# Decoder with two cross attentions: turned scores with the maximum subtracted in the product, low parts of the probabilities on VectorE

## The reference

```python
q = (query @ Wq + bq); k = (bank @ Wk + bk); v = (bank @ Wv + bv)
scores = einsum('bhqd,bhkd->bhqk', q, k) / sqrt(hd)
attn = softmax(scores, axis=-1)
out = einsum('bhqk,bhkd->bhqd', attn, v)
return out @ Wo + bo
```

## Time and profile before

| | |
|---|---|
| median of 3 runs | 2616.53 us (2615.01 to 2621.03) |
| span of the profiled execution | 2613.8 us |
| its mean granted clock | 0.934 |
| busy: PE, VectorE, ScalarE, GpSimd | 2432.4, 1110.8, 947.7, 585.1 us |
| first attention, second attention | 105 to 766 us, 1127 to 1789 us |

### The profile page before, as it was taken

One profiled execution on the slowest core, in us unless ns is written; L12 is line 12 of the kernel. 1 busy time (PEld: TensorE's weight loads), 2 busy tenths in 40 slices (PEclk: granted clock), 3 DMA queues, 4 the chain that ended last, 5 costly groups with the idle time before them and its releaser, 6 DMA issues.

```text
span 2613.8 us, 38193 instructions
## 1 busy us (share of the span) xinstructions
PE 2432.4 (93%) x14208; PEld 2160.2 (83%) x14208; DVE 1110.8 (42%) x2206; ACT 947.7 (36%) x1892; POOL 585.1 (22%) x397
## 2 busy tenths in 40 slices
PE   4899999999977789699999999998999999999997
PEld 3788888888866667588888888887999999999997
DVE  7455545555457368444556455654640000200022
ACT  2444434454443144343454344533222222311130
POOL 4111101110132634311111011101222222222222
PEclk9899999999978878789999999998999999999998
DMA  3000000000021010100100000000111111111111
GB/s 136 1 24 24 15 8 23 23 23 6 22 81 29 1 44 0 60 1 28 28 27 21 6 27 27 32 1 33 64 48 65 56 64 56 56 56 64 56 57 41
DMA packets 29513, 93.60 MB, mean 36 GB/s; under 512 B 3752, under 2 KB 4008, under 8 KB 29320
## 3 DMA queue, kind: packets, MB, share of 16 engines
q1 hardware_dynamic: 29448, 92.72, 11.0%
HBM read 91.07 MB, written 1.64 MB: 35 GB/s over the span
## 4 chain that ended last, share of the span: by engine, by line
PE 86%; DVE 6%; ACT 3%; POOL 3%; issue 2%; DMA 0%; DVEq 0%; SPq 0%; POOLq 0%; ACTq 0%
PE psS L272 18%; PE psS L274 16%; PE psS L273 16%; PE psT L1337 7%; PE psJ L272 4%; PE psJ L273 4%; PE psJ L274 4%; PE psO L272 4%; PE psO L274 3%; PE psO L273 3%; PE psT L272 2%; PE psT L274 2%; PE psT L273 2%; DVE x_res L884 1%; DVE stats L877 1%
## 5 line engine op out<-in xcount | busy, mean ns | idle before, releaser
L272 PE MATMUL psS<-hid_hi,fw_hi 128*128 128x400 f32 x1152 | 398.1, 346 | 15.4 <-DVE hid_lo L1258 10.6
L274 PE MATMUL psS<-hid_hi,fw_lo 128*128 128x400 f32 x1152 | 400.2, 347 | 0.0
L273 PE MATMUL psS<-hid_lo,fw_hi 128*128 128x400 f32 x1152 | 399.6, 347 | 0.0
L529 POOL TENSOR_TENSOR fw_lo<-raw,fw_hi 128x1024 fp32r<-128x1024 f32 x88 | 216.7, 2464 | 572.1 <-ACT fw_hi L751 572.1
L615 ACT ACTIVATE pT_hi<-psT 128x300 fp32r<-128x300 f32 x512 | 187.4, 418 | 263.0 <-PE psT L1337 262.5
L1258 DVE TENSOR_TENSOR hid_lo<-h_act,hid_hi 128x800 fp32r<-128x800 f32 x32 | 32.3, 1083 | 555.6 <-ACT hid_hi L840 555.6
L606 ACT ACTIVATE p<-psS,nmax 100x722 f32<-100x722 f32 x256 | 221.9, 867 | 68.9 <-DVE nmax L928 36.4
L936 DVE TENSOR_TENSOR pT_lo<-psT,pT_hi 128x300 fp32r<-128x300 f32 x512 | 216.4, 464 | 38.1 <-ACT pT_hi L615 32.8
L370 POOL TENSOR_TENSOR cT_lo<-ctx_raw,cT_hi 128x722 fp32r<-128x722 f32 x58 | 102.1, 1761 | 580.0 <-ACT cT_hi L565 580.0
L272 PEld LDWEIGHTS psS<-hid_hi,fw_hi 128*128 128x128 f32 x1152 | 218.0, 189 | 16.4 <-issue 11.2
L272 PE MATMUL psO<-pT_hi,vv_hi 128*64 128x200 f32 (+1 forms) x768 | 219.2, 285 | 2.4 <-DVE oraw L947 2.4
(11 more groups left out here) (306 smaller groups left out, 4909.4 us busy)
## 6 DMA issues: line engine op xcount, KB each, us to landing
raw<-ffn_dram SPq DMA_DIRECT2D x88, 512.0 KB, 3.2
ctx_raw<-ctxT_dram SPq DMA_DIRECT2D x60, 361.0 KB, 3.1
mask_raw<-mask_dram SPq DMA_DIRECT2D x8, 282.0 KB
raw<-wk_dram SPq DMA_DIRECT2D x4, 512.0 KB, 3.5
raw<-wv_dram SPq DMA_DIRECT2D x4, 512.0 KB, 6.6
raw<-wq_dram SPq DMA_DIRECT2D x4, 512.0 KB, 3.3
raw<-wo_dram SPq DMA_DIRECT2D x4, 512.0 KB, 3.2
cin<-xT_dram SPq DMA_DIRECT2D x1, 1600.0 KB, 8.3
```

The lines of the kernel that those rows point to most:

```text
L272: nc.tensor.matmul(out, st[0], mv_[0], start=first, stop=False)
L273: nc.tensor.matmul(out, st[0], mv_[1], start=False, stop=False)
L274: return nc.tensor.matmul(out, st[1], mv_[0], start=False, stop=last)
L529: nc.gpsimd.tensor_tensor(fw.lo[:, e, :], raw[:, e, :], fw.hi[:, e, :], ALU.subtract)\
```

## The change

The scores are computed twice. First as before, queries down and keys along, but only to get the maximum of each query. Then turned, keys down and queries along, with three more rows in the product that carry the negated maximum (its high and low part, against ones), so that the maximum is subtracted in the product, and the exponential comes out in the layout in which the value products need it; the transposes of the probabilities are gone. The three split products of a score become one: the 32 features of a head are stacked three times (high, low and high of the keys against high, high and low of the queries), with a fourth row for the mask in the second attention. For that keys and queries are written to DRAM in parts (`keys_out`, `queries_out`) and loaded again stacked (`keys_in`, `queries_in`); the key tile kS holds two groups of four heads.

ScalarE takes the exponential of a head twice, once to p in fp32 and once, rounded, to pT, and VectorE subtracts the two (`probs_lo`), both now in SBUF. The value products take high values, a block of ones and low values as one stationary operand of 96 columns and the two parts of the probabilities as 200 moving columns; the ones give the sums. `heads_out` adds the two halves out of psO into heads_sum, and a batch ends with `inverse_sums`, `high_values` (ScalarE), `low_values` (GpSimd) and `outputs` in place of the products of lines 1374 and 1379. `context_lo` of two of four chunks moves from GpSimd to VectorE. The loop goes over 8 pairs of heads instead of 17 steps; there is one score tile (psS0) for the first kind of scores, and psS1 and psT hold the turned ones. PE runs ahead by one pair with the first kind. The first batch's group 1 of keys and the first half of group 2 are made ahead of the loop. The weight blocks of the low-rank feed-forward are loaded and split after the first attention, since part of `raw` now holds rinv and lows; the fill values are set by GpSimd in `pads`.

The pieces of the diff that carry this (in full it also renames the semaphores of the two attentions into one set):

```diff
-CONTEXT_AT = {10: 0, 11: 1, 13: 2, 14: 3}
+CONTEXT_AT = {3: (0, 1), 4: (2, 3)}
+KEYS_AT = {0: (2, 1), 1: (3, 0), 2: (3, 1)}
+NEXT_KEYS_AT = {5: (0, 0), 6: (0, 1), 7: (1, 0)}
+PAIRS = H // 2
...
+            def keys_in(L, b, g):
+
+                B = b + NB * L
+                wait_apart(sp, A.kd_out0, 16 * C * B + 16 * (g + 1))
+                wait_apart(sp, A.kd_out1, 16 * C * B + 16 * (g + 1))
+                wait_apart(sp, A.st_mm, H * B + G * (g - 1))
+                for r, x in enumerate((0, 1, 0)):
+                    sp.dma_start(kS[HD * r:HD * (r + 1), g % 2, :, :].bitcast(fp32),
+                                 k_dram[g % 2, :, x, :].rearrange("(j p) n -> p j n", j=G))\
+                      .then_inc((A.ks_in0, A.ks_in1)[g % 2], 16)
+                if L == 1:
+                    sp.dma_start(kS[STACK:STACK + 1, g % 2, :, :].bitcast(fp32),
+                                 mask_dram[bass.ds(b, 1), :].unsqueeze(1).to_broadcast([1, G, KEYS]))\
...
+            def queries_in(L, b, g):
+
+                wait_apart(sp, A.st_mm, H * (b + NB * L) + G * (g + 1) - H)
+                for r, x in enumerate((0, 0, 1)):
+                    sp.dma_start(qS[HD * r:HD * (r + 1), G * g:G * (g + 1), :].bitcast(fp32),
+                                 q_dram[x, :, g, bass.ds(b * T, T)].rearrange("(j p) t -> p j t", j=G))\
+                      .then_inc((A.qs_in0, A.qs_in1, A.qs_in2, A.qs_in3)[g], 16)
...
+                def batch(b, last):
+                    if not last:
+                        context(L, b + 1, (0, 1))
+                    keys_out(L, b, 2, 1)
+                    keys_in(L, b, 2)
+                    if not last:
+                        queries_in(L, b + 1, 0)
+                    keys_out(L, b, 3, 0)
+                    keys_out(L, b, 3, 1)
+                    if not last:
...
+                        context(L, b + 1, (2, 3))
+                    keys_in(L, b, 3)
...
+            sp.wait_ge(A.o_scaled, NB)
...
+            def low_values(L, b):
+
+                B = b + NB * L
+                wait_apart(pool, A.u_done, PAIRS * B + PAIRS)
+                wait_apart(pool, A.resid_done, B + 1)
+                for j in range(G):
+                    r = HD * (1 + j % 2)
+                    wait_apart(pool, A.x_done, G * B + j)
+                    nc.gpsimd.tensor_copy(lows[HD * j:HD * (j + 1), :, :], heads_sum[r:r + HD, j:H:G, :])                      .then_inc(A.x_done, 1)
...
+                def probs(b, h):
+
+                    B, e = b + NB * L, h % 2
+                    act.wait_ge(A.st_mm, H * B + h + 1)
+                    wait(act, A.pt_lo, H * B + h - 1)
+                    nc.scalar.activation(p[:, e, :].rearrange("p (i n) -> p i n", i=2), st_view[e], ACT.Exp,
+                                         scale=SCALE).then_inc(A.exped, 1)
 
...
                 def probs_hi(b, h):
...
+
+                    B, e = b + NB * L, h % 2
+                    if e == 0:
+                        wait(act, A.pv_mm, PAIRS * B + h // 2 - 1)
+                    nc.scalar.activation(pT[:, h % 4, :, 0:T].rearrange("p (i k) t -> p i k t", i=2),
+                                         st_view[e].rearrange("p i (k t) -> p i k t", k=HK), ACT.Exp, scale=SCALE)\
+                      .then_inc(A.pt_hi, 1)
...
+                def max_rows(b, t):
+
+                    act.wait_ge(A.t_mm, PAIRS * (b + NB * L) + t + 1)
+                    nc.scalar.activation(qS[STACK:TROWS, 2 * t:2 * t + 2, :],
+                                         psS[0][0:3, KEYS:KEYS + 2 * T].rearrange("p (e t) -> p e t", e=2), ACT.Copy)\
+                      .then_inc(A.rows_set, 1)
+
...
+                    for t in range(PAIRS):
+                        probs(b, 2 * t)
+                        probs_hi(b, 2 * t)
+                        if t in KEYS_AT:
+                            keys_hi(L, b, *KEYS_AT[t])
+                        if t in NEXT_KEYS_AT and not last:
+                            keys_hi(L, b + 1, *NEXT_KEYS_AT[t])
+                        if t in CONTEXT_AT:
+                            if not last:
+                                context_hi(L, b + 1, CONTEXT_AT[t][0])
+                            probs(b, 2 * t + 1)
+                            max_rows(b, t + 1)
+                            probs_hi(b, 2 * t + 1)
+                            if not last:
+                                context_hi(L, b + 1, CONTEXT_AT[t][1])
+                        else:
+                            if t < PAIRS - 1:
+                                max_rows(b, t + 1)
+                            probs(b, 2 * t + 1)
+                            probs_hi(b, 2 * t + 1)
                     if not last:
...
+                    nc.vector.tensor_reduce(nraw[:, h % 2:h % 2 + 1], psS[0][0:T, 0:KEYS], AX.X, ALU.max, negate=True)\
+                      .then_inc(A.maxed, 1)
...
+                def probs_lo(b, h):
+
+                    dve.wait_ge(A.pt_hi, H * (b + NB * L) + h + 1)
+                    nc.vector.tensor_tensor(pT[:, h % 4, :, T:2 * T], p[:, h % 2, :].rearrange("p (k t) -> p k t", k=NKC),
+                                            pT[:, h % 4, :, 0:T], ALU.subtract).then_inc(A.pt_lo, 1)
...
+                def heads_out(b, t):
+
+                    dve.wait_ge(A.pv_mm, PAIRS * (b + NB * L) + t + 1)
+                    nc.vector.tensor_reduce(heads_sum[:, 2 * t:2 * t + 2, :],
+                                            psO[0:STACK, 0:4 * T].rearrange("p (e x t) -> p e t x", e=2, x=2), AX.X,
+                                            ALU.add).then_inc(A.u_done, 1)
...
+                    for t in range(PAIRS):
+                        if t >= 2:
+                            heads_out(b, t - 2)
+                        if t < PAIRS - 1:
+                            head_max(b, 2 * t + 2)
+                        probs_lo(b, 2 * t)
+                        if t < PAIRS - 1:
+                            head_max(b, 2 * t + 3)
+                            max_parts(b, t + 1)
+                        if t in KEYS_AT:
+                            keys_lo(L, b, *KEYS_AT[t])
+                        if t in NEXT_KEYS_AT and not last:
+                            keys_lo(L, b + 1, *NEXT_KEYS_AT[t])
+                        probs_lo(b, 2 * t + 1)
+                        if t == 0 and not first:
+                            norm_stats(base + b - 1, 0, y[:, 0, :])
+                        if t == 2 and not first:
+                            norm_apply(base + b - 1, 0, y[:, 0, :], b - 1)
+                        if t in CONTEXT_AT and not last:
+                            context_lo(L, b + 1, CONTEXT_AT[t][1])
...
+                    wait(pe, A.maxed, H * B + h)
+                    for k0, kn in PIECES:
+                        if k0 and h % 2 == 0:
+                            wait(pe, A.rows_set, PAIRS * B + h // 2)
+                        mm = nc.tensor.matmul(psS[0][0:T, k0:k0 + kn], qS[0:SROWS, h, :],
+                                              kS[0:SROWS, g % 2, j, k0:k0 + kn], start=True, stop=True)
+                    mm.then_inc(A.s_mm, 1)
...
+                def scores_turned(b, h):
...
+                    wait(pe, A.pt_hi, H * B + h - 1)
+                    for k in range(NKC):
+                        n = key_rows(k)
+                        k0 = KA * (k // HK) + T * (k % HK)
+                        mm = nc.tensor.matmul(st_bank[h % 2][0:n, k0:k0 + T], kS[0:TROWS, g % 2, j, KC * k:KC * k + n],
+                                              qS[0:TROWS, h, :], start=True, stop=True)
+                    mm.then_inc(A.st_mm, 1)
...
+                def weighted(b, h):
...
+                    pe.wait_ge(A.pt_lo, H * B + h + 1)
+                    if e == 0:
+                        wait(pe, A.u_done, PAIRS * B + t)
...
+                        mm = nc.tensor.matmul(psO[0:STACK, 2 * T * e:2 * T * (e + 1)], vv[0:n, k, t, 2 * HD * e:2 * HD * e + STACK],
+                                              pT[0:n, h % 4, k, :], start=k == 0, stop=k == NKC - 1)
+                    if e == 1:
+                        mm.then_inc(A.pv_mm, 1)
...
+                    for t in range(PAIRS):
+                        if t < PAIRS - 1:
+                            scores(b, 2 * t + 2)
+                        scores_turned(b, 2 * t)
                         if t >= 1:
...
+                            weighted(b, 2 * t - 2)
+                        if t < PAIRS - 1:
+                            scores(b, 2 * t + 3)
+                        if t in KEYS_AT:
+                            keys(L, b, *KEYS_AT[t])
+                        if t in NEXT_KEYS_AT and not last:
+                            keys(L, b + 1, *NEXT_KEYS_AT[t])
+                        scores_turned(b, 2 * t + 1)
+                        if t in CONTEXT_AT:
+                            weighted(b, 2 * t - 1)
+                        if t < PAIRS - 1:
+                            max_turned(b, t + 1)
```

(28 more changed lines are left out.)

703 lines of the change are left out of this document (359 added, 344 removed).

## The result

The changed kernel took 2872.92 us (median of four runs, 2863.33 to 2885.09) against 2615.77 for the kernel before, beside it: a ratio of 1.0975, with a 95% interval of 1.0939 to 1.1011. The forecast was 2785 in a range of 2540 to 2920 with slower at 0.78. So direction and range held, and the time was 88 us further up than the forecast.

The account below looks back on a forecast made before the run. PE was taken to bound the kernel, a batch being its own work. Batches going from 84.0 to 92.3 us give +133, work outside them 35: 2613.8 + 2.7 + 133 + 35 = 2785 us, range 2540 to 2920.

Parts of the forecast that it names:

- PE is relieved: In the pairs, PE's work per head falls from 2.66 to 1.7 us, 15 us less per batch, but goes into waits.
- The circle: In a pair of heads, waits through PE, ScalarE and VectorE close a loop of twelve terms: 7.6 us a pair.
- The clock: In the pairs, short products and waits lower PE's granted clock to 0.79: 8 us a batch.
- The rival that the clock holds: In attention, waits too short to lower the clock: a batch of 84.3 us, 2657 us in all; chance 0.18.
- The faster rival: Pairs closing sooner, 2332 us at the most, halfway 2490; decides below a pair of about 6.2 us; chance 0.20.
- The slowest rival: Half clock through the pairs, or key loads late in each batch: 2960 us; chance 0.10.
- The tail: At a batch's end, PE's own work alone, 25.7 us, and 1.5 where it begins slow.
- Outside the batches: Ahead of each attention 10 us of stores, loads and maxima, together 20; 15 at the feed-forward's start.
- The key loads: In the loop, stacked loads land in 6 us; the fourth group's come about 1 us late, hidden under another wait.

Follow-up runs that it names:

- e2_dve: Changed kernel with VectorE taking the sum of psO and the next maximum ahead of the low part of the pair's second head; 2702.2 us.
- e5_keys: Changed kernel with PE's key block moved ahead of the value products of each pair's first head; 2770.0 us.
- e7_pool_lo: Changed kernel with all low parts of the probabilities on GpSimd in place of VectorE; 2735.1 us.
- e4_fill: Changed kernel with eight extra products of 360 columns, result overwritten, ahead of the value products of each pair's first head; 2816.9 us.
- c1_both: Changed kernel with the VectorE order of e2_dve and the single reciprocal of e1_rinv, the reciprocal behind the next batch's maxima; 2637.8 us.
- c2_split: c1_both with the fourth key group's stacked loads in two halves, the first issued a pair earlier; 2550.8 us, ratio 0.9743 to the kernel before.
- e1_rinv: Changed kernel with one reciprocal over 128 partitions in place of four over 32, after four more ScalarE copies; 2798.1 us.
- e3_sp: Changed kernel with the fourth key group's loads ahead of the load of context chunk 3 on SyncE's queue; 2879.3 us.

## Why the prediction was right, and by how much it was off

- **PE is relieved, and its saving goes into waits.** Right. PE is busy 80% of the attention's time (319.21 of 400 us), forecast 75.
- **The circle, 7.6 us a pair.** Right in its mechanism, shown by e2_dve, e5_keys and e7_pool_lo; 7.11 us measured. Each term came out within 0.15: both exponentials 0.57 from start to start and 0.69 with the hand-over (0.70 and 0.66 forecast), low part 0.70 to the next start and 0.78 by itself (0.78), sum 0.56 (0.55), maximum 0.91 (0.92 with its start), turned head 0.57 (0.60), key block 2.01 (2.05). The forecast was the sum of estimates that each were a little dear. A turned product took 0.57 / 6 = 0.095 us: the row of the nearest shape was the better price, and the rule of the Trainium skill (TensorE: Matmul & The Clock Gate, LDWEIGHTS) with 0.107 us does not fit this trace.
- **The clock, 0.79 in the pairs.** Right: the eight pairs of two batches have 0.79 (323.44 to 387.49) and 0.75 (419.12 to 486.09), the tails between and behind them 0.89. The price of 8 us a batch is not measured by itself. It is at least 56 / 16 = 3.5 us by e4_fill; a mean of 0.79 over 64 us is 27 us at half speed, and even if PE had worked all of them, its work would have been 13 us shorter at full speed (both are estimates from these rows). The pairs took 64.1 and 67.0 us where 58.6 + 6.5 = 65.1 were forecast. That agreement is partly luck, since at least two errors in it cancel: pairs at full clock are shorter than forecast, and pair 5 has a wait for key loads that was forecast as hidden:

```profile
464.30 0.92 PE L1503 MATMUL psS<-kS,qS 97*100 97x512 f32 x2 [4.04 <-DMA kS<-k_parts]
```

- **The rival that the clock holds** fell: no wait of PE in the loop is longer than 4.7 us, most are near 2, and the granted clock is 0.69 among them. The section of the Trainium skill that the prediction read for this rival (same page, Why this matters for your kernels) warns of long idle gaps between bursts; by that warning alone this loss would have been missed. e4_fill shows it the other way round: with the waits filled the clock is 0.92.
- **The faster rival's point**, a pair of about 6.2 us, was put too high, in part by the same omission as in the next point: with pairs of 5.34 us e2_dve is still at 2702 us. It takes the single inverse (c1_both, 2638) and the earlier key loads (c2_split, 2551) to get below the kernel before. The slowest rival did not come: half clock does not last through a batch (0.79 and 0.75 in the pairs of the two batches above, and 0.65 in the slow pairs at the start of the first attention, 126 to 190 us).
- **The tail, 25.7 us plus 1.5 for a slow start: here is the step that failed.** The prediction's sentence that the tail is PE's own work left VectorE's inverses out of the sum. Measured are 31.6 (387.49 to 419.12) and 31.8 us (486.09 to 517.93), 4.5 more than 27.2: PE's wait of 3.64, and a value chunk at half clock (12 x 0.20 = 2.4) of which 1.5 were allowed. Fourteen batches have such a tail, since the last one of each attention prepares no next one: 63 us. The profiled execution is 94 us longer than its forecast (2876.1 against 2613.8 + 133 + 35 = 2781.8; the medians differ by 88), and e1_rinv, with one inverse for four, won 75. The trace of before had the operation, on 16 elements per partition:

```profile
750.18 0.25 DVE L969 RECIPROCAL rinv<-rsum 100x16 f32<-100x16 f32 x1
```

  The change gives it 400 elements per partition in each of four pieces, and no term was made of it. No range for an unknown price was put on it either.
- **Outside the batches, 20 + 15 us.** The feed-forward's start was 18.3 later (15 forecast). The last batch of each attention, which had no term of its own, has PE wait 14.31 and 13.71 us for the inverses' result where it waited 2.45 and 1.84 before:

```profile
882.89 0.75 PE L299 MATMUL psO<-wqo_hi,oT_hi 128*100 128x512 f32 x1 [14.31 <-DVE oT_lo L1159]
...
914.44 2.90 PE L1476 MATMUL psS<-ident,x_res 100*128 100x100 f32 x16 [25.15 <-DVE xT_lo L1033]
918.54 0.70 PE L299 MATMUL psS<-xT_hi,u_hi 128*128 128x400 f32 x1 [1.20 <-DVE xT_lo L1033]
```

  The wait of 25.15 us is put down to the transposed values, but these were late for another reason. In the chain of waits the loads of the weight blocks and their splits stand one behind the other, as forecast, and the transposed values come on ScalarE only behind them (913.20 us):

```profile
907.53 4.68 DMA raw<-rq_dram
912.24 1.06 ACT rqo_hi L671
```

  The starts of the attentions were dearer than 10 us each:

```profile
115.38 0.89 PE L1503 MATMUL psS<-kS,qS 97*100 97x512 f32 x2 [9.98 <-DMA qS<-q_parts]
...
126.09 0.49 PE L1511 MATMUL psS<-ident,nmx 100*3 100x100 f32 x2 [6.07 <-DVE nmx L1089]
```

  The first wait, 9.98, is the one forecast (queries out, back in). The second, 6.07, is new, and the rows for it are in the last section. The loop itself (its first score product) begins 23.1 us later than before in the first attention (126.29 against 103.17) and 23.2 us in the second, where 143.3 of 1294.89 against 1128.35 had gone before; that is more than twice the forecast; part of it is a key block that was made inside the loop before. This is the second term that was too small: up to the first batch's projection the two attentions are 43.8 and 30.5 us longer, where 8.3 + 10 were forecast for each. So of the 94 us some 38 arose there, 52 between the first and the last projections (80.6 and 87.1 us longer, 58.1 forecast for each), and the rest at the feed-forward's start and the ends; the fourteen tails are spread over the first two.
- **The key loads** take 7.1 us from issue to landing in the chain (457.08 to 464.19), forecast 6. That they do no harm was wrong where pairs are short (87 us in c2_split against c1_both), and open where they are long: in the changed kernel PE waits 58.3 us for them, in 14 of 16 batches; e3_sp removed most of that wait without gain but held up the context load in exchange, and the halved loads were not tried without the other two moves.

## What to carry to other kernels

When a change takes work off the engine that bounds, walk the new order of waits through all engines before counting the saving: here the work taken off PE, 15 us a batch by the forecast, turned into waits, and an exchange of two operations on VectorE was worth 171 us. Price every instruction that the change gives a new shape, also in the part of the loop that looks like the bounding engine's own work. And judge the engine for an operation only in the right order: the same move to GpSimd won 138 us in one order and lost 22 in the other.

## What the runs showed of the hardware

An inverse costs by the elements of a partition, whatever the number of partitions: 2.64 us for 32 x 400 and 2.65 for 128 x 400, 0.25 for 100 x 16, so some 6.2 ns an element, over four times the sum's (0.57 us for 400).

VectorE's smallest operations can be the most delayed ones. At the start of the attention, VectorE and then GpSimd:

```profile
121.77 1.98 DVE L1087 CAST nmx<-nraw 100x2 fp32r<-100x2 f32 x1
123.78 2.26 DVE L1089 TENSOR_TENSOR nmx<-nraw,nmx 100x2 f32<-100x2 f32 x1
```

```profile
121.38 4.64 POOL L476 TENSOR_TENSOR wqo_lo<-raw,wqo_hi 128x1024 fp32r<-128x1024 f32 x2 [33.73 <-ACT wqo_hi L671]
```

A copy and a subtraction of 100 x 2 values, 0.17 us each at the median, take 1.98 and 2.26 us while GpSimd subtracts two blocks of 1024 columns, 2.3 us each; each of the two ends within 0.1 us of the end of a block. They are 4.2 of the 6.07 us of the wait above; the rest is the keys' low part and the maximum ahead of them. It fits the Trainium skill (SBUF — State Buffer, Who interferes with whom), by which a VectorE operation with two inputs in SBUF, or a cast in a fast mode, and one of GpSimd that reads SBUF hold the same port for a whole instruction each; no run here took the two apart. The maximum and the sum, which read PSUM, kept their time: in e7_pool_lo, with GpSimd busy for 143 us of the 400 between 300 and 700 in place of 43, they take 0.906 and 0.566 us in the mean, in the changed kernel 0.905 and 0.565, while the copy goes from 0.32 to 0.82 and the subtraction from 0.16 to 0.36.
